# Where a layer norm's small steps run: offset, mean and reciprocal moved from GpSimd to VectorE, the root moved up in GpSimd's queue

## The reference

```python
def _layernorm(x, axis=-1, eps=1e-05):
    m = jnp.mean(x, axis=axis, keepdims=True)
    v = jnp.var(x, axis=axis, keepdims=True)
    return (x - m) / jnp.sqrt(v + eps)
...
        q = shape_heads((hidden_states @ wq.T + bq) * scaling)
        k = shape_heads(hidden_states @ wk.T + bk)
        v = shape_heads(hidden_states @ wv.T + bv)
        scores = jnp.einsum('bhtd,bhsd->bhts', q, k)
        mask = jnp.triu(jnp.full((T, T), -10000.0, dtype=jnp.float32), k=1)
        attn = jax.nn.softmax(scores.astype(jnp.float32) + mask, axis=-1).astype(jnp.float16)
        out = jnp.einsum('bhts,bhsd->bhtd', attn, v)
        out = out.transpose(0, 2, 1, 3).reshape(B, T, E)
        return out @ wo.T + bo
...
        logits = xt @ Ws + bs
        topk_w, topk_idx = jax.lax.top_k(logits, K)
        topk_w = jax.nn.softmax(topk_w, axis=-1)
        combine = jnp.sum(jax.nn.one_hot(topk_idx, E, dtype=xt.dtype) * topk_w[..., None], axis=1)
        g = jnp.einsum('td,edf->tef', xt, Wg)
        u = jnp.einsum('td,edf->tef', xt, Wu)
        h = jax.nn.silu(g) * u
        y = jnp.einsum('tef,efd->ted', h, Wd)
        out = jnp.einsum('ted,te->td', y, combine)
...
    x = x + _layernorm(_L0_attn_ref(_layernorm(x, axis=-1), ...), axis=-1)
    x = x + _layernorm(_L0_ffn_ref(_layernorm(x, axis=-1), ...), axis=-1)
```

## Time and profile before

| | |
|---|---|
| median of 3 runs | 888.92 us (882.98 to 889.88) |
| profiled execution, its own time | 890.5 us |
| its span, first to last instruction | 888.7 us |
| granted TensorE clock, mean | 0.908 |
| busy: PE, DVE, ACT, POOL | 718.2, 635.0, 536.3, 434.0 us |

### The profile page before, as it was taken

How to read it: one execution, slowest core, us unless ns; L and a number is a source line. 1 busy time by engine, 2 the same in 40 slices (tenths; PEclk the granted TensorE clock), 3 DMA queues, 4 the chain that set the end, 5 groups by cost and what they waited for, 6 DMA issues and landing times. The chain is left out here.

```text
span 888.7 us, 22060 instructions
## 1 busy us (share of the span) xinstructions
PE 718.2 (81%) x6822; PEld 471.2 (53%) x6823; DVE 635.0 (71%) x2034; ACT 536.3 (60%) x1086; POOL 434.0 (49%) x515
## 2 busy tenths in 40 slices
PE   3476787778788899979998998889885999999930
PEld 1144444445443355545554564567773878778720
DVE  5777898889877988887897778467551556556545
ACT  4688875867656676756765674665642444344427
POOL 3563432644534556774675467577352233242228
PEclk9889997989985799999988997899996999999975
DMA  6435232463332101221112111223335233233248
GB/s 192 136 118 153 82 113 71 126 194 116 112 130 63 43 14 26 50 48 26 26 28 53 19 32 34 41 40 57 50 86 137 37 44 46 36 47 42 30 113 291
DMA packets 72812, 68.91 MB, mean 78 GB/s; under 512 B 6800, under 2 KB 66320, under 8 KB 72720
## 3 DMA queue, kind: packets, MB, share of 16 engines
q1 hardware_dynamic: 59440, 53.23, 19.7%
q0 software_dynamic: 13280, 14.49, 11.6%
HBM read 34.04 MB, written 31.29 MB: 74 GB/s over the span
## 5 line engine op out<-in xcount | busy, mean ns | idle before, releaser
L944 ACT ACTIVATE pT<-bank 128x512 f16<-128x512 f32 (+1 forms) x384 | 200.3, 534 | 100.1 <-PE bank L1521 98.7
L728 POOL TENSOR_SCALAR_AFFINE_SELECT pT<-pT 128x512 f16<-128x512 f16 x128 | 88.2, 734 | 144.7 <-ACT pT L944 144.4
L1087 DVE TENSOR_REDUCE nmax<-bank 128x1 f16<-128x384 f32 (+2 forms) x216 | 126.1, 597 | 34.7 <-PE bank L1510 33.3
L1944 POOL DMA_INDIRECT expert_rows<-y_sb,dest x36 | 56.0, 1554 | 120.1 <-DVE y_sb L2063 114.6
L1100 DVE CUSTOM_DVE_ANT_0 unused<-bank,mask 128x384 f16<-128x384 f32 (+2 forms) x224 | 103.6, 483 | 14.4 <-PE bank L1499 12.8
L2138 PE MATMUL bank<-xT,gu_part 128*128 128x256 f16 (+1 forms) x792 | 95.9, 280 | 2.6 <-issue 1.7
L1614 PE MATMUL bank<-tile_xT,gu_part 128*128 128x256 f16 (+1 forms) x616 | 90.9, 289 | 8.5 <-DVE stage L1284 8.4
L2138 PEld LDWEIGHTS bank<-xT,gu_part 128*128 (+1 forms) x792 | 78.5, 102 | 19.0 <-issue 4.2
L1552 PEld LDWEIGHTS bank<-va,pT 128*128 128x128 f16 x1280 | 55.4, 99 | 51.1 <-issue 27.8
L1552 PE MATMUL bank<-va,pT 128*128 128x17 f16 x1280 | 68.0, 174 | 15.8 <-POOL pT L728 15.8
L162 POOL DMA_INDIRECT dispatch_rows<-rows,slot x64 | 66.9, 1046 | 21.5 <-issue 16.7
(11 more groups left out here) (218 smaller groups left out, 1618.6 us busy)
## 6 DMA issues: line engine op xcount, KB each, us to landing
expert_rows<-tile_in SPq DMA_DIRECT2D x8, 1024.0 KB, 6.2
stage<-wg SPq DMA_DIRECT2D x8, 688.0 KB, 4.2
stage<-wu SPq DMA_DIRECT2D x8, 688.0 KB, 4.2
stage<-wd SPq DMA_DIRECT2D x8, 640.0 KB, 4.3
gu_part<-expert_rows SPq DMA_DIRECT2D x16, 256.0 KB, 5.7
out<-gu_part SPq DMA_DIRECT2D x16, 256.0 KB, 2.9
tile_in<-dispatch_rows SPq DMA_DIRECT2D x21, 130.0 KB, 2.2
rows<-dispatch_rows SPq DMA_DIRECT2D x18, 130.0 KB, 2.2
```

The lines of the kernel that those rows point to most:

```text
L728: last = gp.affine_select(out=diagonal, in_=diagonal, compare_op=ALU.is_ge, fill=0.0, base=0, pattern=[[0, J], [1, P]], channel_multiplier=-1)
L944: sc.activation(pT[:, lo:hi], ST_BANK[i % 2][:, 0:hi - lo], ACT.Exp, scale=1.0 / INV_SCALE).then_inc(p_ready, 1)
L1087: v.tensor_reduce(columns, S_BANK[i % 2][:, 0:n * len(heads)].rearrange("p (j n) -> p j n", n=n), AX.X, ALU.max, negate=True).then_inc(s_m ...
```

## The change

The offset and the mean are computed on DVE right behind the moments. POOL keeps one power of 0.5. The reciprocal is taken on DVE with its own instruction, at the start of the first half of the scaling. In POOL's loop the root of group 1 moves ahead of the second mask, and that of group 2 ahead of the stores of a tile.

```diff
--- before.py
+++ after.py
@@ -210,7 +210,7 @@
         mine_row = sb(stack, "mine_row", [P, G, E], F32)
         rowf = sb(stack, "rowf_early", [P, G], F32)
         used = sb(stack, "used", [P, E], F32)
-        power = sb(stack, "power", [P, 2, QT], F32)
+        power = sb(stack, "power", [P, QT], F32)
         iota8 = sb(stack, "iota8", [P, E], F32)
         x_sb = sb(stack, "x_sb", [P, QT, D], F16)
         xr_sb = sb(stack, "xr_sb", [P, QT, D], F16)
@@ -660,17 +660,11 @@
                 gp = nc.gpsimd
                 def rsqrt(n):
 
-                    pool.wait_ge(var_ready, n + 1)
-                    gp.tensor_scalar(veps[:, :], mv[:, :, 1], LN_EPS16, None, ALU.add).then_inc(veps_ready, 1)
-                    gp.tensor_copy(mean[:, :], mv[:, :, 0]).then_inc(mean_ready, 1)
                     pool.wait_ge(veps_ready, n + 1)
-                    gp.tensor_tensor(std[:, :], veps[:, :], power[:, 0, :], ALU.pow).then_inc(std_ready, 1)
-                    pool.wait_ge(std_ready, n + 1)
-                    gp.tensor_tensor(rstd[:, :], std[:, :], power[:, 1, :], ALU.pow).then_inc(rstd_ready, 1)
+                    gp.tensor_tensor(std[:, :], veps[:, :], power[:, :], ALU.pow).then_inc(std_ready, 1)
 
                 ch = Chain(pool, pool_const, spare)
-                ch.link(gp.memset(power[:, 0, :], 0.5))
-                ch.link(gp.memset(power[:, 1, :], -1.0))
+                ch.link(gp.memset(power[:, :], 0.5))
                 ch.link(gp.memset(ones[:, :], 1.0))
                 ch.link(gp.memset(clear, 0.0))
                 any_f = dict(allow_small_or_imprecise_dtypes=True)
@@ -764,18 +758,18 @@
                             at = (g, c)
                             if at == (0, 0) and not in_last:
                                 rsqrt(1 if first else 3 * b - 1)
+                            if at == (1, 1) and not first:
+                                rsqrt(3 * b - (1 if in_last else 0))
                             cut(G * b + g, c)
                             n = G * b + g - FIRST_TILE
                             if n >= 0:
                                 tile_low(n, c)
+                            if at == (2, 0) and not first:
+                                rsqrt(3 * b + 1 - (1 if in_last else 0))
                             if n >= 1 and c == 0:
                                 store_tile(n - 1)
                             if n >= -1 and c == 1:
                                 take_tile(n + 1)
-                            if at == (1, 1) and not first:
-                                rsqrt(3 * b - (1 if in_last else 0))
-                            if at == (2, 0) and not first:
-                                rsqrt(3 * b + 1 - (1 if in_last else 0))
                             if first and c == 0:
                                 low_part(PIECES_AT[b, g][0])
                             if at in AT_SCATTER and scattering:
@@ -1059,11 +1053,16 @@
                     for t in range(QT):
                         last = v.bn_aggr(mv[:, t, :], stats[:, t, :])
                     last.then_inc(var_ready, 1)
+                    hold(dve, var_ready, n + 1, spare)
+                    v.tensor_scalar(veps[:, :], mv[:, :, 1], LN_EPS16, None, ALU.add).then_inc(veps_ready, 1)
+                    v.tensor_copy(mean[:, :], mv[:, :, 0]).then_inc(mean_ready, 1)
 
                 def norm_scale(dst, src, n, half):
                     if half == 0:
+                        dve.wait_ge(std_ready, n + 1)
+                        v.reciprocal(rstd[:, :], std[:, :]).then_inc(rstd_ready, 1)
                         dve.wait_ge(mean_ready, n + 1)
-                        dve.wait_ge(rstd_ready, n + 1)
+                        hold(dve, rstd_ready, n + 1, spare)
                     for t in HALVES[half]:
                         last = v.tensor_scalar(dst[:, t, :], src[:, t, :], mean[:, t:t + 1], rstd[:, t:t + 1],
                                                ALU.subtract, ALU.mult)
```

## The result

| | before | after |
|---|---|---|
| median of 4 runs each, in one session | 889.4 us (882.98 to 890.87) | 908.61 us (906.87 to 913.21) |
| ratio | | 1.0215, 95% interval 1.0171 to 1.0259 |
| profiled execution: span, mean granted clock | 888.7 us, 0.908 | 905.0 us, 0.895 |

The change costs 19.2 us. The forecast was 899, slower by 1.1%: the right side, but half the size. 908.61 lies outside the 894 to 904 that the forecast had for itself and 0.4 us inside the whole range, so that it fell inside is luck.

A forecast was written before the change was run, and what follows sets the result against it. Neither PE nor POOL is full, so waits decide. Terms 4 + 7.8 + 1.2 - 0.8 = 12.2 us, less a fifth 9.8, give 900.3, by the median 899 us; own range 894 to 904, whole 884 to 909.

The forecast's parts named there:

- first moved root: Group 1, second mask: the root now ahead of the selects delays PE's mask, +7.8 us over seven batches, bounds +4 to +9.
- start and gap: Kernel start, constants ready earlier but memsets later, -0.3; between 600 and 650 us, earlier POOL stores, -0.5; together -0.8 us.
- a fifth off: Whole sum: PE's delays partly fall into following waits for ACT or DVE, so 12.2 us becomes 9.8.
- What comes on DVE: All norms: added small operations cost 0.65 us each, 16 in all; +4 us on the path, bounds 0 and +10.
- second moved root: Group 2, first step: root ahead of a tile's stores, masks behind it lose 1.35 us of POOL work; +1.2 us, bounds -4, +4.
- A rule weighed: Scalings at 396.50 took 1.52 us beside POOL's selects; by the shared-port rule less POOL work frees DVE; part of rival 1.
- rival 1: POOL's shorter chain wins if the second mask's new order costs nothing: -8.2 us, about 881 us; chance 0.14.
- The signs: Profile after: mask waits about 20 us, step 10 waits 1.2 or more, maxima +2 to 4, POOL -34, DVE +12.
- Rival 2: Waits for DVE and ACT absorb DVE's 4 us and half of the first moved root's 7.8: 893 us; chance 0.24.
- Rival 3: Stalls cost PE clock: one more stretch at 1.2 GHz adds 5 us, 904 us; chance 0.10.

The follow-up runs named there:

- the third kernel: Changed kernel with both roots back at their places of before, leaving only the split of operations between DVE and POOL: 895.99 us, ratio 1.0073.
- the one with one power: Kernel before with one power of -0.5 on POOL replacing root and power of -1, nothing more on DVE, order as before: 877.71 us, ratio 0.9873.

## Why the prediction was right on the side and wrong in size

By its own working, the prediction's 12.2 us split into the same parts that the runs measured:

| part | predicted us | measured us |
|---|---|---|
| VectorE's additions (4, and 4 x 0.35 inside the first moved root) | 5.4 | 13.6 (12.1 to 15.1) |
| mask's order, without those 0.35 | 6.4 | 8.6, uncertain by 4 |
| stores' order (0.7 + 1.35 each in batches 5 and 6, 0.7 in 7) | 4.8 | 5.3, uncertain by 3 |
| POOL's relief, with start and gap | -4.4 | -7.1, uncertain by 3 |
| sum | 12.2 | 20.4 |
| a fifth off | -2.4 | |
| change | 9.8 | 19.2 |

The first four measured rows are differences between four of the kernels. Their sum exceeds the change by 1.2 us, well within their uncertainty. The first row alone is 8.2 of the 9.4 us by which the forecast fell short.

**What comes on DVE** is the step that failed. The unit was right (0.35 predicted, 0.38 in the rows); how often it is paid, and what follows from it, was not. Working from a profile in which PE's waits for DVE "come every few steps up to 280 us and rarely behind", I took 0.6 us in three batches, 0.3 in three later ones and 0.2 for each of seven reciprocals, and let the rest hide. Groups 0 of batches 1 to 6 show 3.4 us for the 2.7, so that part was nearly right. The reciprocals and moments of group 2, priced at 1.4, show 5.6 in six batches (with clock in it). Batch 0 (2.0 us) and groups 2 and 3 of batch 4 (5.2) have 10.2 and 15.3 us more of low clock, which the term did not contain at all; by PE's busy time the clock is about 5 us of all that the additions cost. The bound of 10 was too low: the 16 that the same paragraph named as DVE's whole new work was the upper end to keep.

**The first moved root** held up to its details. Predicted +7.8 with DVE's part; groups 1 show +10.3, less 2.5 given back at once in batches 3 and 4, which is 7.8. There the mask's wait (1.31 us in batch 3) was added, and the next wait for the maxima took most of it back, as the step on the earlier trace rows had it. The wait of batches 1 and 2 is 1.17 and 1.26 us (1.2 or more was asked, so batch 1 falls just short), that of batches 5 and 6 3.03 (3.0).

**The second moved root** was priced at 2.05 a batch for the order in batches 5 and 6, and the delays there were 1.60 and 1.61; in batch 7 it was 1.85 against 0.7. The relief set against it was larger in turn: with start and gap in it, the two rows of the table come to -1.8 for +0.4, the same within their uncertainty. Start and gap, priced at -0.8, show -1.3 and -3.1 in the pair of profiles; the same program's two profiles already differ by 1.1 behind attention.

**A fifth off** for delays that fall into other waits has nothing to stand on in the runs: the 2.5 us that were given back in groups 1 had been counted already, and the measured parts leave 1.2 us at most for it, within the uncertainty.

**A rule weighed** read one row wrongly. The pair of scalings at 396.50 did not take 1.52 us because POOL ran its selects beside them: the selects ended at 396.81, and the long one of the pair (1.20 us, from 396.82) ran beside the low part at 396.78. There are three such scalings of 1.20 us before, in batches 5 to 7, where rival 1 counts four pairs.

**The signs.** PE's waits for masks 19.9 (about 20), POOL -33.9 (-34), DVE +11.6 (+12), POOL's wait stands ahead of the root: all as said. The maxima +5.9 instead of 2 to 4: this one, small as it looks, told of the term that failed. The waits for rows grew by 2.8 us in all (5.9 before).

**The rivals.** The shorter chain was worth nearly what rival 1 gave it (7.1 of 8.2 us), and one power shows it without the additions: 11.3 us for 24 us less on POOL, where the relief of the split gave 7.1 for 31.6. So a relief of POOL has no fixed price either. In both (the third kernel and the one with one power) the scalings of 1.20 us in batches 5 and 6 are gone, as rival 1 wanted. But the second mask cost 8.6 us where it had to be near nothing. Rival 2, hidden, is out. Rival 3, with 904 the nearest of the times, had a real mechanism: a price of 5 us was put on one more stretch of low clock, and a stretch of 10.2 us cost 4.4 in one program's two profiles, and 6.8 us more in group 3 of batch 5 cost 2.45. How much of the 19 us is clock cannot be told exactly, since only the kernel before has a second profile; the groups 2 and 3 of batches 4, 5 and 7 suggest 6 to 8 us of 16.3 in the pair compared here, and PE's busy time, longer by 8.4 us, agrees.

## What to carry to other kernels

When two engines hand small work to each other in order queues, price an operation by what stands queued behind it: on POOL a root of 1.05 us ahead of a mask delayed the group by 1.07 to 1.61 us in each of seven batches, though POOL was half idle, and only in two of them half or more of it came back. An engine that is waited for every few steps (DVE's maxima) has little slack for 0.4 us insertions; take their whole sum as the bound, and look first for a way to drop an operation instead of moving it, as one power for two did. And add a price for the clock to a sum of new stalls.

## What the runs showed of the hardware

- One program, profiled twice, kept the same times within 0.33 us a group, and differed by 4.44 us in one group through 10.2 us at the lower clock. A difference of that size between two profiles need not come from an edit.
- A wait of DVE for its own last aggregate costs about as much as the small operation behind it: the offset starts 0.51 to 0.54 us after the aggregates started in nearly all 24 norms, where an independent reduce of the kernel before started after 0.28 to 0.30; the offset itself takes 0.19.
- Scalings on DVE and the selects and low part on POOL all have longer records where they run at the same time. In batch 5 one scaling of 128x256 took 1.20 us beside the low part before and 2.14 beside selects and low part after (median 0.38), the pair of selects 1.23 and 1.80, the low part 1.16 and 1.71. The Trainium skill (SBUF — State Buffer, "Who interferes with whom") has, with DVE in a two-port mode, the one that comes second blocked for the whole instruction of the other. The rows show both sides stretched in their records, and no run here separates which one waited.
- A power on 128x4 takes POOL 1.05 us with an exponent of 0.5 or -0.5 and 1.01 with -1, so among these three the exponent is free to choose.
